# Row and column attention with residual: x and out tiled by row pairs, the middle tile computed in two column halves of the array

## What is computed

```python
msa = jnp.transpose(x, (0, 2, 1, 3))
sw = jax.nn.softmax(QKs, axis=-1)                       # weights over the 128 rows
Q = (x @ Wq).reshape(B, R, C, H, D) * scaling * sw
K = (x @ Wk).reshape(B, R, C, H, D)
V = (x @ Wv).reshape(B, R, C, H, D)
QK = jnp.einsum('brihd,brjhd->bhij', Q, K)
attn = jax.nn.softmax(QK, axis=-1)
out = jnp.einsum('bhij,brjhd->brihd', attn, V)
return x + out.reshape(B, R, C, E)                      # x here is the input before the normalisation
```

## Time and profile before

| what | value |
|---|---|
| median of three runs | 583.38 us (578.85 to 587.22) |
| profiled execution (its span) | 583.2 us |
| PE busy | 516.6 us (89%), 5167 matmuls |
| DVE, ACT, POOL busy | 394.4 us, 313.4 us, 243.0 us |
| DMA | 134.30 MB, mean 230 GB/s; 168224 of 183447 packets are under 512 B |
| chain that ended last | PE 68%, DVE 14%, DMA 7%, POOL 3%, ACT 2%, ACTq 2% |

### The profile page before, as it was taken

One profiled execution on the slowest core, in us unless ns is written; L12 is line 12 of the kernel. 1 busy time (PEld: TensorE's weight loads), 2 busy tenths in 40 slices (PEclk: granted clock), 3 DMA queues, 4 the chain that ended last, 5 costly groups with the idle time before them and its releaser, 6 DMA issues.

```text
span 583.2 us, 13858 instructions
## 1 busy us (share of the span) xinstructions
PE 516.6 (89%) x5167; PEld 390.0 (67%) x5167; DVE 394.4 (68%) x989; ACT 313.4 (54%) x646; POOL 243.0 (42%) x280
## 2 busy tenths in 40 slices
PE   7697685799999999999899996694999979999893
PEld 5687542355555555455499985494999979998783
DVE  3599767577878777778836686372467663667873
ACT  4477665597999999995412130332456650223231
POOL 2000231755777777774300033572455660002583
PEclk9898899699999999999999999698899998999997
DMA  8997012444666666787699999988777739999998
GB/s 327 384 417 268 2 55 108 163 145 128 217 217 218 215 202 209 200 211 161 120 286 270 269 297 312 320 226 246 256 254 251 258 96 241 303 286 278 309 258 230
DMA packets 183447, 134.30 MB, mean 230 GB/s; under 512 B 168224, under 2 KB 170080, under 8 KB 183392
## 3 DMA queue, kind: packets, MB, share of 16 engines
q1 hardware_dynamic: 132384, 113.80, 63.2%
q10 hardware_dynamic: 51008, 19.76, 13.3%
HBM read 76.92 MB, written 56.62 MB: 229 GB/s over the span
## 4 chain that ended last, share of the span: by engine, by line
PE 68%; DVE 14%; DMA 7%; POOL 3%; ACT 2%; ACTq 2%; issue 2%; SPq 1%; POOLq 0%; DVEq 0%
PE PS L1175 23%; PE PS L1183 13%; PE PS L1271 7%; DVE EXTRA L765 5%; DMA EXTRA<-in_x 4%; PE PS L1301 3%; PE PS L1305 3%; PE PS L1304 3%; PE PS L1303 3%; PE PS L1302 3%; DVE BIG L1040 3%; ACTq L739 2%; POOL BIG L514 2%; DMA out_x<-EXTRA 1%; PE PS L1136 1%
## 5 line engine op out<-in xcount | busy, mean ns | idle before, releaser
L1175 PE MATMUL PS<-WP,EXTRA 128*128 128x384 f16 (+1 forms) x1152 | 159.9, 291 | 8.0 <-DMA EXTRA<-xt_scratch 8.0
L1175 PEld LDWEIGHTS PS<-WP,EXTRA 128*128 128x128 f16 x1152 | 99.3, 99 | 54.9 <-issue 18.8
L514 POOL TENSOR_TENSOR BIG<-BIG,EXTRA 64x512 f32<-64x512 f32 x36 | 45.1, 1265 | 135.6 <-DVE BIG L1040 111.7
L1271 PE MATMUL PS<-BIG,EXTRA 128*128 128x256 f16 x768 | 89.5, 280 | 12.4 <-ACT EXTRA L745 12.4
L471 POOL TENSOR_TENSOR EXTRA<-BIG,EXTRA 128x512 f16<-128x512 f32 x69 | 81.3, 1180 | 42.4 <-ACT EXTRA L578 34.4
L1271 PEld LDWEIGHTS PS<-BIG,EXTRA 128*128 128x128 f16 x768 | 76.4, 100 | 24.7 <-issue 13.2
L1183 PE MATMUL PS<-WP,EXTRA 64*128 64x384 f16 (+1 forms) x1152 | 90.5, 288 | 0.9 <-DVE EXTRA L904 0.9
L477 POOL TENSOR_TENSOR BIG<-EXTRA,BIG 128x192 f16<-128x192 f32 x96 | 53.6, 559 | 49.4 <-ACT BIG L636 49.4
L1183 PEld LDWEIGHTS PS<-WP,EXTRA 64*128 64x128 f16 x1152 | 44.6, 95 | 30.1 <-issue 18.9
L745 ACT ACTIVATE EXTRA<-PS,small 64x512 f32<-64x512 f32 x48 | 31.3, 682 | 60.8 <-PE PS L1271 19.9
L1040 DVE SCALAR_TENSOR_TENSOR BIG<-PS,small,BIG 128x512 f32<-128x512 f32 x72 | 48.9, 738 | 20.5 <-PE PS L1271 20.5
(11 more groups left out here) (177 smaller groups left out, 953.3 us busy)
## 6 DMA issues: line engine op xcount, KB each, us to landing
EXTRA<-in_x SPq DMA_DIRECT2D x28, 768.0 KB, 8.5
xt_scratch<-EXTRA SPq DMA_DIRECT2D x24, 768.0 KB, 3.4
EXTRA<-xt_scratch SPq DMA_DIRECT2D x24, 768.0 KB, 4.3
v_scratch<-EXTRA SPq DMA_DIRECT2D x32, 384.0 KB, 3.9
BIG<-v_scratch SPq DMA_DIRECT2D x16, 768.0 KB, 6.7
BIG<-in_x SPq DMA_DIRECT2D x12, 768.0 KB, 9.5
out_x<-BIG ACTq DMA_DIRECT2D x12, 768.0 KB, 6.4
v_scratch<-EXTRA SPq DMA_DIRECT2D x32, 192.0 KB, 3.9
```

What stands on the lines that cost most here:

```text
L514: pool.tensor_tensor(o, o, OLOW[j % 3][0:E1, :].rearrange("p (r e) -> p r e", r=RI), ALU.add).then_inc(s_lo[h], 1)
L1175: ins = mm(outs[a], xt[:, t, s, q * P:(q + 1) * P], WP[:, t, w, wc], start=first and j == 0, stop=last and j == 2, skip_group_check=True)
L1271: ins = mm(po[:, :, a, :], stationary, moving, start=j == 0, stop=j == len(terms) - 1)
```

## The change

Two rows of x together have 384 columns, which are three tiles of 128 partitions: the even row's first 128 columns, the odd row's last 128, and between them a middle tile of the even row's last 64 and the odd row's first 64. x and out are loaded, kept and stored in such tiles (`by_thirds`, order outer, outer, middle), so XO has three parts of 128 partitions x 8 row pairs x 96.

- The first step of a block (outer) makes both outer tiles in one bank: per head and parity five matmuls of 128 moving columns (8 rows x 16), 20 in all, with 128 stationary columns.
- The second step (middle) has, per head, five pairs of matmuls. Each has 64 stationary columns and 128 moving columns. One of a pair writes partitions 0..63 (even rows), the other partitions 64..127 (odd rows), 20 in all. All five terms are summed in PSUM.
- OLOW with ACT's copies, POOL's adds and the semaphores `s_ol` and `s_lo` is gone. DVE adds 128 x 512 and then 128 x 256 per block.
- The stores go from ACT's queue to SP's, after all loads of the half, three DMAs per group.
- V has a buffer for each of the eight groups, so V of groups 6 and 7 waits for nothing.
- XO of groups 6 and 7 lies over XT[3] alone: three XT chunks are loaded ahead, one waits for the last store. x of group 6 for h = 1 is loaded right behind that chunk instead of after the projection.
- The low part of the attention matrix is kept in plain order, so one subtraction per head replaces two.

```diff
+    def by_thirds(flat, n, h):
+        thirds = flat[n * RI * C:(n + 1) * RI * C, h * EH:(h + 1) * EH].rearrange("(q t p) e -> p t q e", t=3, p=P)
+        return [thirds[:, t, :, :] for t in (0, 2, 1)]
...
+        VW, XW = RI * EH, RI * EH * 3 // 2
+        FREE = XW + XW
+        V0_AT = [k * HEADW for k in range(HALF)] + [FREE, 2 * HEADW + FREE]
+        V1_AT = [k * HEADW + VW for k in range(HALF)] + [HEADW + FREE, HEADW + FREE + VW // 2]
...
+        at_x7 = ring + 3 * CHUNK
+        XO = XO + [EXTRA[:, at_x7 + XW:at_x7 + 2 * XW], EXTRA[:, at_x7:at_x7 + XW]]
+        XO = [q.rearrange("p (t q e) -> p t q e", t=3, e=EH) for q in XO]
...
             sp.wait_ge(s_pj[0], NG0)
-            for b in range(2):
+            for b in range(3):
                 load_xt(b, b)
...
+                for t, third in enumerate(by_thirds(xf, n, h)):
+                    sp.dma_start(XO[n][:, t, :, :], third).then_inc(s_xl[n], 16)
+
+            def store_out(h, n):
+                sp.wait_ge(s_ad[h], 2 * closes[n] + 1)
+                for t, third in enumerate(by_thirds(of, n, h)):
+                    if t == 2:
+                        sp.wait_ge(s_ad[h], 2 * closes[n] + 2)
+                    sp.dma_start(third, XO[n][:, t, :, :]).then_inc(s_out[n], 16)
...
                 if h:
-                    for k in (6, 7):
-                        sp.wait_ge(s_out[k], 32)
-                    for b in range(2, 4):
-                        load_xt(b, b)
+                    sp.wait_ge(s_out[7], 48)
+                    load_xt(3, 3)
+                    sp.wait_ge(s_out[6], 48)
+                    load_x(1, 6)
...
-                for n in range(NRC - NV):
-                    sp.wait_ge(s_av[h], 2 * closes[n] + 2)
-                    load_v(h, n + NV)
+                for n in range(HALF, NRC):
+                    load_v(h, n)
+                for n in range(NRC):
+                    store_out(h, n)
...
-                for j, (n, hp) in enumerate(BLOCK):
-                    pool.wait_ge(s_ol[h], j + 1)
-                    pool.wait_ge(s_ad[h], 2 * j + 2)
-                    o = XO[X_AT[n]][0:E1, 1, :, hp * 2 * D:(hp + 1) * 2 * D]
-                    pool.tensor_tensor(o, o, OLOW[j % 3][0:E1, :].rearrange("p (r e) -> p r e", r=RI),
-                                       ALU.add).then_inc(s_lo[h], 1)
...
-                for j in range(NB):
-                    act.wait_ge(s_av[h], 2 * j + 2)
-                    when(act, s_lo[h], j - 2)
-                    nc.scalar.activation(OLOW[j % 3][0:E1, :], PS[E1:P, attended_bank(2 * j + 1), :], ACT.Copy,
-                                         scale=mxb[0:E1, WV:WV + 1]).then_inc(s_ol[h], 1)
-                    if j - 2 in closes:
-                        store_out(h, closes.index(j - 2))
-                store_out(h, NRC - 1)
...
-                    for lo, hi, to in ((P, C, C), (0, P, C + E1)):
-                        ins = v.tensor_tensor(AT[:, k, :, to:to + hi - lo], pa[:, :, lo:hi],
-                                              AT[:, k, :, lo:hi], ALU.subtract)
+                    ins = v.tensor_tensor(AT[:, k, :, C:2 * C], pa, AT[:, k, :, 0:C], ALU.subtract)
...
+                    v.scalar_tensor_tensor(outer, PS[:, attended_bank(2 * j), :].rearrange("p (r e) -> p r e", r=RI),
+                                           mxb[:, WV:WV + 1], outer, ALU.mult, ALU.add).then_inc(s_ad[h], 1)
+                    dve.wait_ge(s_av[h], 2 * j + 2)
+                    v.scalar_tensor_tensor(middle, PS[:, attended_bank(2 * j + 1), 0:256]
+                                           .rearrange("p (q e) -> p q e", e=2 * D),
+                                           mxb[:, WV:WV + 1], middle, ALU.mult, ALU.add).then_inc(s_ad[h], 1)
...
+                po = PS[:, attended_bank(m), :].rearrange("p (t q a d) -> p t q a d", t=2, a=2, d=D)
+
+                def terms(k, odd, columns):
+                    high, low = AT[:, k, :, columns], AT[:, k, :, C:2 * C][:, :, columns]
+                    v0h, v0l = (V0[n][:, odd:RI:2, s, k * D:(k + 1) * D] for s in range(2))
+                    v1 = V1[n][:, odd:RI:2, k * D:(k + 1) * D]
+                    return ((high[:, 0, :], v0h), (high[:, 0, :], v0l), (low[:, 0, :], v0h),
+                            (high[:, 1, :], v1), (low[:, 1, :], v1))
+
                 for a in range(2):
                     k = 2 * hp + a
                     if t == 0:
...
+                        for odd in range(2):
+                            for i, (stationary, moving) in enumerate(terms(k, odd, I_LAST if odd else I_FIRST)):
+                                ins = mm(po[:, odd, :, a, :], stationary, moving, start=i == 0, stop=i == 4)
                     else:
...
+                        for i, pair in enumerate(zip(terms(k, 0, slice(P, C)), terms(k, 1, slice(0, E1)))):
+                            for odd, (stationary, moving) in enumerate(pair):
+                                ins = mm(po[odd * E1:(odd + 1) * E1, 0, :, a, :], stationary, moving,
+                                         start=i == 0, stop=i == 4)
```

More of the change, by code:

```diff
@@ L69, in raw @@
             return RAW[:, lo:lo + n, (c // 2) * P:(c // 2 + 1) * P]
[L71 to L76, removed]
+        VW, XW = RI * EH, RI * EH * 3 // 2
+        FREE = XW + XW
+        V0_AT = [k * HEADW for k in range(HALF)] + [FREE, 2 * HEADW + FREE]
+        V1_AT = [k * HEADW + VW for k in range(HALF)] + [HEADW + FREE, HEADW + FREE + VW // 2]
+        V0 = [BIG[:, at:at + VW].bitcast(fp16).rearrange("p (r s e) -> p r s e", s=2, e=EH) for at in V0_AT]
+        V1 = [BIG[:, at:at + VW // 2].bitcast(fp16).rearrange("p (r e) -> p r e", e=EH) for at in V1_AT]
+        XO = [BIG[:, k * HEADW + XW:k * HEADW + FREE] for k in range(HALF)]
         EXTRA = sb("EXTRA", [P, 15104])
@@ L241, in row_column_attention @@
         s_atl = [sem(f"attention_lows{h}") for h in range(2)]
-        s_vl = [sem(f"v_loaded{k}") for k in range(NV)]
+        s_vl = [sem(f"v_loaded{k}") for k in range(NRC)]
         s_xl = [sem(f"residual_loaded{k}") for k in range(NRC)]
@@ L246, in row_column_attention @@
         s_ad = [sem(f"residual_added{h}") for h in range(2)]
-        s_ol = [sem(f"attended_low_part{h}") for h in range(2)]
-        s_lo = [sem(f"low_part_added{h}") for h in range(2)]
         s_out = [sem(f"out_stored{k}") for k in range(NRC)]
@@ L341, in row_column_attention @@
         closes = [max(j for j in range(NB) if BLOCK[j][0] == n) for n in range(NRC)]
[L343 to L348, removed]
+        I_FIRST, I_LAST = slice(0, P), slice(E1, C)
         block = ctx.enter_context(nc.Block())
@@ L431, in _ @@
                     sp.wait_ge(s_pj[1], NG1)
-                load_x(h, 6)
+                else:
+                    load_x(0, 6)
                 load_x(h, 7)
-                for n in range(NV):
+                for n in range(HALF):
                     sp.wait_ge(s_qk[h], n + 1)
@@ L1030, in _ @@
                 attention_low(HALF - 1)
[L1033 to L1041, removed]
+                for j, (n, hp) in enumerate(BLOCK):
+                    if opens[n] == j:
+                        dve.wait_ge(s_xl[n], 48 * (h + 1))
+                    o = XO[n][:, :, :, hp * 2 * D:(hp + 1) * 2 * D]
+                    dve.wait_ge(s_av[h], 2 * j + 1)
+                    outer, middle = o[:, 0:2, :, :].rearrange("p t q e -> p (t q) e"), o[:, 2, :, :]
+                    v.scalar_tensor_tensor(outer, PS[:, attended_bank(2 * j), :].rearrange("p (r e) -> p r e", r=RI),
[4 more added lines that the diff above has]
+                                           mxb[:, WV:WV + 1], middle, ALU.mult, ALU.add).then_inc(s_ad[h], 1)
         @block.tensor
```

51 lines of the change are left out of this document (10 added, 41 removed).

## The result

| | median | profiled execution |
|---|---|---|
| kernel before | 582.12 us (578.64 to 589.81, 20 runs) | 583.2 us |
| changed kernel | 576.64 us (571.44 to 582.48, 20 runs) | 576.2 us |

By these medians it is 5.5 us less. The ratio is 0.9885, with a 95% interval of 0.9852 to 0.9917; this ratio, like those of the experiments, is formed from the runs in the faster of two states alone, so it differs a little from that of the medians (0.9906). The forecast was 568 us, 15 us less. The sign was right, and less than half of the gain came.

What follows compares the result with a forecast made beforehand. It took DMA, through the last store's landing, to set half 0, and PE to pace the second AV stage. 583.2 − 12.7 (between the halves) − 3.1 (second half and tail) = 567.4, given as 568 us, range 562 to 590.

Steps and rivals of the forecast that it cites:

- What bounds the kernel: Reading of the kernel before: ACT's store issue starves PE, PE waits for the last store between halves, DMA nearly always busy.
- ACT's stall: First half, 358.9 us: ACT spends 10.1 us in one store issue; ending it worth nothing unless the stores end earlier too.
- PE: AV stage: a block of outer and middle steps takes 1.90 us, 0.16 more than now, if middle pairs run at once.
- the changes of shape: AV stage on PE: two switches between array shapes per block, 0.11 us each, 0.22 us together.
- the rival of exposed loads: Middle step: weight loads not hidden behind matmuls, PE becomes the bound in both halves; from 595 us, chance 0.10.
- DVE: AV stage: DVE's two adds take 0.74 and about 0.42 us, 1.16 us per block, covered by PE's 1.90.
- Loads: Half 0: groups 0 to 5 follow every 7.93 us instead of 8.53; the loads end at 361.6 us.
- Stores: Half 0, behind the loads on SP: eight groups at 3.7 us end at 391.2 us, landed at about 393.2.
- The rival with the transfers as before: The 64 partitions are not what slows stores, DMA as before; 578 us, no change, chance 0.12.
- Between the halves: Last store to fifth projection chunk: XT[3] load, x of group 6, chunk load; fifth chunk at 403.1 us, gain 12.7 us.
- Half 1 and tail: Second AV stage ends at 573.2 us (old clock) against 573.92; tail 6.9 us instead of 9.3; gain 3.1 us.

Runs made afterwards that it cites:

- long runs: Changed kernel with each partition's row of a store as one run of 3072 bytes in DRAM instead of eight of 384: 564.02 us, ratio 0.969.

## Why the prediction was wrong, by its own steps

**What bounds the kernel: right.** That the landing of the last store sets half 0, and not ACT's stall, is shown by the kernel before with its stores on SP: the stall went and the time stayed.

**PE: right.** 1.90 us a block were forecast and 1.90 measured; the changes of shape cost 0.12 us each, forecast 0.11. The loads of 64 columns take 110 ns and those of 128 columns 98, and both stay hidden, so the rival of exposed loads is out. With it falls, for this case, the rule of the Trainium skill (TensorE: Matmul & The Clock Gate, Part 3) that a load overlaps only where the rows differ: both halves of a pair use all 128 rows, and ten pairs take 0.68 us.

**DVE: right in what matters.** The two adds take 0.75 and 0.48 us a block, forecast 0.74 and 0.42, under PE's 1.90.

**Loads: right.** V of a group follows every 7.96 us, forecast 7.93. They begin 2.1 us later in this execution (the first XT load is issued at 294.62 us; 292.54 in before), which the stages ahead brought and the change doesn't touch, and end near 365 us, 1.3 us more behind that start than forecast. That end isn't sharp, since the first store is issued at 359.63 us, among the last loads.

**Stores: the step that failed.** "Eight at 3.7 us end at 391.2, landed at about 393.2." From the end of the loads to the last landing 31.6 us were forecast, and 37.1 came. The 3.7 us rest on 320 GB/s, which I read from the best stretches of stores that ran alone at the end of the kernel. A stream of stores holds 284 GB/s, 4.15 us a group, so eight groups take 3.6 us more than forecast. The other 1.9 us lie where loads and stores overlap and where the last store runs out; the rows don't divide them further. At the end of the changed kernel, where the last group stands alone, it is faster than in the stream, but not by that much (40 slices of 568 to 576.2 us, 0.205 us each):

```profile
DMA  9999643211129999999999999999997100000000
GB/s 305 305 307 225 142 88 67 51 36 36 37 67 303 324 283 255 326 319 315 328 322 272 292 318 317 320 317 313 305 290 169 26 17 17 13 0 0 0 0 0
```

The last group takes 19 slices, 3.9 us, at a mean of some 300 GB/s. The falling stretch that each group of the earlier trace rows has, with the DMA engines busy all through it, isn't there. Where the rate falls here, at the end of group 6, the engines fall idle with it. So the stretch did belong to the 64-partition part. But of the 0.6 us that I took off each of 16 transfers per half for it, the loads gave 0.4 to 0.6 (8.53 us a group in before and 8.37 with its stores on SP, 7.96 now), a group of stores alone 0.4 (4.3 to 3.9), and one in a stream 0.25 (4.40 to 4.15). So the best rate of a lone transfer was taken for that of eight behind each other. Why a stream is slower than a lone group wasn't tried.

The rival with the transfers as before (578 us) came out nearest, but partly by luck: its reason fell, since loads and stores are faster without the 64-partition part, and 2.1 us of its nearness are the late start, which is in none of its terms.

**Between the halves.** From the last landing to the fifth chunk 9.9 us were forecast and 10.6 came. I had PE do three chunks by itself; I overlooked that ACT waits for the stores of groups 0 to 5 before it copies K. PE therefore stops after two chunks (24 full matmuls and 24 in row halves each) and takes up work again at a lower clock. Behind the 7.22 us in which it stood still the granted clock is 0.50, the 1.2 GHz level (the third chunk's 24 full matmuls in 4.00 instead of 2.15 us):

```profile
396.48:400.41 3.93, 3.93 (x24) 3.45 (x25) 1.84 (x6) 0.83 (x2) 2.17 (x3) 0.50 0.99 243
```

It cost little, because PE had to wait for XT[3] anyway (4.59 us behind it, and another 0.88 for the fifth chunk's load). With long runs, where the stores are early, this wait isn't there.

**Half 1 and tail: right.** 164.3 us from the fifth chunk on were forecast, 163.4 came; the tail was 6.85 us for 6.9.

The sum of the errors: start 2.1, loads 1.3, stores 5.5 (the term that was mis-sized), between the halves 0.7, half 1 −0.9. That is 8.7 us, and 567.4 + 8.7 = 576.1, where the profiled execution has 576.2.

## What to carry to other kernels

Where DMA is busy all the time, ask of every removed wait what the engine will wait for next, and find the transfer that lands last: here a stall of 10.4 us and a wait of 8 became a wait of 20.5. Take the rate of a stream of transfers from a stream of the same kind, not from the best stretch of one that runs alone. Bytes that needn't move (data that is still in place), together with a better order of what lies over what, were worth more here than a quicker order of the matmuls.

## What was unexpected in the hardware

Stores of 384-byte runs hold 279 to 289 GB/s when several follow each other, even while PE and DVE stand still, and some 300 when a group stands alone; with runs of 3072 bytes, which also lie without gaps, they hold 406 to 413. Stores of 64 partitions, one behind the other, begin at 213 to 218 GB/s and go on at 256; where only a third of the bytes is in them, the stream holds 268. None of these differences was traced to its cause. Matmuls that write different column halves overlap even when five of one half are issued ahead of five of the other: 0.76 us for 20, where one after the other would be 1.12 (20 times the 55.8 ns that the outer step bears out: 1.22 us with its change of shape).
